# Output in token rows, and a base loaded in token rows and scaled by GpSimd, in a two-layer attention kernel

## What is computed

```python
# layer 0: per image, xn = group-normalised x, channels by tokens
q, k, v = Wq@xn + bq, Wk@xn + bk, Wv@xn + bv
out = softmax(q.T @ k) applied to v
y   = sigmoid(relu(mean(xn) @ se_w1.T) @ se_w2.T)     # one number per channel
x   = x + gamma*out + xn*y                            # the "base" is x + xn*y
# layer 1: tokens by channels
t = x as tokens (the image transposed)
t = t + softmax(n @ n.T) @ n                          # n = layer-normalised t
p = softmax(ln(t) @ router_w + router_b); the best 2 of 8 experts, renormalised
t = t + sum over the 2 experts of p_e * (ln(t) @ expert_w[e] + expert_b[e])
return t as image (transposed back)
```

## Time and profile before

| | |
|---|---|
| median of 3 runs | 2607.51 us (2606.56 to 2609.67) |
| span of the profiled execution | 2606.9 us |
| TensorE (PE) busy | 2524.8 us, 97% |
| VectorE (DVE) busy | 2123.7 us, 81% |
| ScalarE (ACT) busy | 1843.8 us, 71% |
| GpSimd (POOL) busy | 455.6 us, 17% |
| loads of x | 24 of 384 KB, 4.2 us from issue to landing |
| stores of y | 48 of 192 KB, 1.9 us |

### The profile page before, as it was taken

The page is one execution under the profiler, slowest core; times in us unless marked ns, Lnnn a source line. Parts: engine busy times, 40 slices in busy tenths (PEclk is TensorE's granted clock), DMA queues, the critical chain, the costliest instruction groups (busy, mean ns, idle before and its releaser), DMA issues.

```text
span 2606.9 us, 45676 instructions
## 1 busy us (share of the span) xinstructions
PE 2524.8 (97%) x15201; PEld 2325.1 (89%) x15201; DVE 2123.7 (81%) x6221; ACT 1843.8 (71%) x3598; POOL 455.6 (17%) x840
## 2 busy tenths in 40 slices
PE   6999999999999999999999999999999999999997
PEld 5889998899988999889988899889998899988996
DVE  6896789878888788887888878988779877898776
ACT  4667766777677776777766777667776777767775
POOL 0000221013210131101311014010240112300134
PEclk9999999999999999999999999999999999999998
DMA  1000000000000000000000000000000000000000
GB/s 39 1 19 1 4 10 1 22 4 7 7 1 22 4 7 7 16 8 4 10 4 22 1 4 10 4 22 1 4 10 4 22 1 4 13 1 4 1 10 13
DMA packets 11319, 23.12 MB, mean 9 GB/s; under 512 B 1360, under 2 KB 7760, under 8 KB 11088
## 3 DMA queue, kind: packets, MB, share of 16 engines
q1 hardware_dynamic: 11088, 20.20, 2.2%
HBM read 10.76 MB, written 9.44 MB: 8 GB/s over the span
## 4 chain that ended last, share of the span: by engine, by line
PE 72%; DVE 13%; ACT 8%; issue 5%; POOL 1%; DMA 1%; SPq 0%; ACTq 0%; POOLq 0%; DVEq 0%
PE ps L1193 19%; PE ps L1195 19%; PE ps L1194 19%; PE ps L1213 11%; DVE row_space L997 4%; ACT row_space L740 2%; DVE pt_lo L1012 2%; PE ps L1338 2%; ACT row_space L792 1%; DMA x_chan<-x 1%; DVE pt_lo L1092 1%; ACT pt_hi L751 1%; DVE t_tok L1030 1%; ACT pt_hi L801 1%; DVE xg_lo L957 1%
## 5 line engine op out<-in xcount | busy, mean ns | idle before, releaser
L751 ACT ACTIVATE pt_hi<-ps 128x384 fp32r<-128x384 f32 x864 | 419.9, 489 | 290.3 <-PE ps L1213 287.4
L1012 DVE TENSOR_TENSOR pt_lo<-ps,pt_hi 128x384 fp32r<-128x384 f32 x864 | 473.6, 551 | 108.7 <-ACT pt_hi L751 102.6
L997 DVE TENSOR_SCALAR_CACHE_REDUCE row_space<-ps,key_bias 128x512 f32<-128x512 f32 (+1 forms) x720 | 492.4, 690 | 52.8 <-PE ps L1195 48.4
L1213 PE MATMUL ps<-ident,row_space 128*128 128x128 f32 x2736 | 448.4, 273 | 20.9 <-ACT row_space L740 20.9
L740 ACT ACTIVATE row_space<-row_space,negmax 128x512 f32<-128x512 f32 (+2 forms) x432 | 403.0, 933 | 64.6 <-DVE negmax L1006 64.4
L1213 PEld LDWEIGHTS ps<-ident,row_space 128*128 128x128 f32 x2736 | 344.7, 141 | 105.0 <-ACT row_space L740 34.3
L1193 PE MATMUL ps<-pt_hi,v_hi 128*128 128x384 f32 x864 | 355.8, 412 | 8.4 <-ACT y_out L760 7.7
L1092 DVE TENSOR_TENSOR pt_lo<-row_space,pt_hi 128x768 fp32r<-128x768 f32 x260 | 251.0, 966 | 96.1 <-ACT pt_hi L801 96.1
L792 ACT ACTIVATE row_space<-ps,shift 128x768 f32<-128x768 f32 x260 | 233.9, 900 | 127.7 <-PE ps L1195 126.6
L1193 PE MATMUL ps<-pt_hi,tn_hi 128*128 128x384 f32 x864 | 304.6, 353 | 9.8 <-DVE pt_lo L1092 6.9
L1194 PE MATMUL ps<-pt_lo,tn_hi 128*128 128x384 f32 x864 | 292.5, 339 | 0.0
(11 more groups left out here) (210 smaller groups left out, 5453.6 us busy)
## 6 DMA issues: line engine op xcount, KB each, us to landing
x_chan<-x SPq DMA_DIRECT2D x24, 384.0 KB, 4.2
y<-y_out SPq DMA_DIRECT2D x48, 192.0 KB, 1.9
t_tok<-eb SPq DMA_DIRECT2D x1, 516.0 KB, 5.5
t_tok<-ew SPq DMA_DIRECT2D x1, 516.0 KB, 6.3
row_space<-wqkv SPq DMA_DIRECT2D x1, 192.0 KB, 3.3
se_sb<-se SPq DMA_DIRECT2D x1, 68.0 KB, 4.8
biases<-channel SPq DMA_DIRECT2D x1, 2.0 KB, 5.1
```

Source lines behind the costliest of these rows:

```text
L751: act.activation(pt_hi[:, slot, :], ring_bank(step)[:, 0:BW], ACT.Copy)\
L997: dve.tensor_scalar(row_part(n, r, a, w), ring_bank(step)[:, 0:w], key_bias[:, row:row + 1], None, ALU.add, ALU.max, accum_out=mx[:, row % ...
L1012: dve.tensor_tensor(pt_lo[:, slot, :], ring_bank(step)[:, 0:BW], pt_hi[:, slot, :], ALU.subtract).then_inc(pt_lo_ready, 1)
L1213: ins = pe.transpose(ring_bank(step)[:, k * 128:(k + 1) * 128], src(k), ident[:, :])
```

## The change

`x` is passed a second time as `tokens`, in token rows, laid out by the host. SP loads it straight into `t_tok`, in two parts (tiles 0 to 11 and 12 to 17), the first when the last `expert` of block 3 of the image before is done, the second when its last `o1add` is. GpSimd multiplies each block by the scale and adds the shift, in the place of `baset`. For that the two columns are turned into rows spread over all partitions: a new step `rows` (VectorE spreads them, TensorE transposes twice, ScalarE copies out). The steps `base` and the transposes and copies of `baset` are gone. The output is stored in token rows from `acc`, which now has two buffers; `yt` and `y_out` are gone, the -1 is put into the shift, and the host transposes the result. Loads of the next x wait for `xgnorm` in place of `baset`.

```diff
@@ EARLIER_BLOCK
-                 4: {4: [('expert', 2)], 9: [('scaled', 2)], 15: [('yt',)]}}
+                 4: {4: [('expert', 2)], 9: [('scaled', 2)]}}
@@ moe: the step yt and its slots (22, 35, 44, 49, 58, ...) are dropped
@@ PROJECT_SLOTS
-                 16: [('base', 0)], 18: ...
-                 22: [('base', 1)], 35: [('base', 2)]}
+                 16: [('rows', 0)], 18: ...
@@ FIRST_BLOCK
-FIRST_BLOCK = {0: [('fold', 0)], 1: [('fold', 1)], 4: [('fold', 2), ('foldsplit',)], 5: [('base', 0)], 8: [('base', 1)],
-               9: [('base', 2)]}
+FIRST_BLOCK = {0: [('fold', 0)], 1: [('fold', 1)], 4: [('fold', 2), ('foldsplit',)], 5: [('rows', 0)]}
@@ sync
+            def load_tokens(b, u):
+                tiles = slice(0, 4 * TPB) if u == 0 else slice(4 * TPB, NT)
+                sp.dma_start(t_tok[:, tiles, :], tokens[b][:, tiles, :]).then_inc(tokens_loaded[u], 16)
+
+            sp.wait_ge(e_split, 2)
+            load_tokens(0, 0)
+            load_tokens(0, 1)
+
             def store(b, mb):
-                sp.wait_ge(y_chan_ready, at(y_chan_ready, "yt", b, mb))
-                sp.dma_start(y[b, :, mb * BW:(mb + 1) * BW], y_out[:, out_buffer(mb), :]).then_inc(y_stored[out_buffer(mb)], 16)
+                sp.wait_ge(tile_added, at(tile_added, "scaled", b, mb, TPB - 1))
+                sp.dma_start(y[b, mb], acc[:, mb % 2, :, :]).then_inc(y_stored[mb % 2], 16)
             for b in range(B):
                 if b + 1 < B:
-                    sp.wait_ge(ring_full, filled(("baset", b, NB - 1)))
+                    sp.wait_ge(xg_norm_ready, at(xg_norm_ready, "xgnorm", b, LB - 1))
...
                 for mb in range(4):
                     store(b, mb)
                 if b + 1 < B:
+                    sp.wait_ge(expert_added, at(expert_added, "expert", b, 3, TPB - 1))
+                    load_tokens(b + 1, 0)
+                    sp.wait_ge(o1_added, at(o1_added, "o1add", b, NB - 1))
+                    load_tokens(b + 1, 1)
                     store(b, 4)
@@ gpsimd
+                if kind == "baset":
+                    m = step[2]
+                    t = t_tok[:, TPB * m:TPB * (m + 1), :]
+                    shape = [128, TPB, 128]
+                    pool.wait_ge(base_rows_ready, at(base_rows_ready, "rows", b, 0))
+                    pool.wait_ge(tokens_loaded[m // 4], 16 * (b + 1))
+                    pool.tensor_tensor(t, t, base_rows[:, 0, :].unsqueeze(1).broadcast_to(shape), ALU.mult)\
+                        .then_inc(base_scaled, 1)
+                    pool.wait_ge(base_scaled, at(base_scaled, *step))
+                    pool.tensor_tensor(t, t, base_rows[:, 1, :].unsqueeze(1).broadcast_to(shape), ALU.add)\
+                        .then_inc(base_tok_ready, 1)
@@ scalar: base, baset and yt dropped
+                elif kind == "rows":
+                    act.wait_ge(ring_full, filled(step))
+                    if b:
+                        act.wait_ge(base_tok_ready, at(base_tok_ready, "baset", b - 1, NB - 1))
+                    act.activation(base_rows[:, :, :], tiled(ring_bank(step)[:, 0:256]), ACT.Copy).then_inc(base_rows_ready, 1)
@@ vector
+                elif kind == "rows":
+                    if b:
+                        dve.wait_ge(ring_full, filled(("rows", b - 1, 0)))
+                    dve.tensor_copy(rows_src[:, :, :], gs[:, 9:11].unsqueeze(2).broadcast_to([128, 2, 128])).then_inc(rows_spread, 1)
@@ vector, expert, k == 0
-                        if b or m:
+                        if b or m >= 2:
-                            dve.wait_ge(ring_full, filled(("yt", *block_before(b, m))))
+                            dve.wait_ge(y_stored[m % 2], 16 * (b * (NB // 2) + m // 2))
@@ tensor
-                elif kind == "baset":
-                    m = step[2]
-                    pe.wait_ge(base_done, at(base_done, "base", b, m // 2))
-                    transpose3(step, lambda k: x_chan[:, m * BW + k * 128:m * BW + (k + 1) * 128])
+                elif kind == "rows":
+                    wait_ring(step)
+                    pe.wait_ge(rows_spread, at(rows_spread, *step))
+                    for k in range(2):
+                        ins = pe.transpose(ring_bank(step)[:, k * 128:(k + 1) * 128], rows_src[:, k, :], ident[:, :])
+                    ins.then_inc(ring_full, 1)
...
-                elif kind == "yt":
-                    m = step[2]
-                    pe.wait_ge(tile_added, at(tile_added, "scaled", b, m, TPB - 1))
-                    transpose3(step, lambda k: acc[:, k, :])
```

More of the change, by code:

```diff
@@ L113, in statistics, with moe @@
                                                   ("se_in", b), ("se_out", b)]
-def moe(b, m, norm, ut, router, experts, out):
-    s = {router: [("router", b, m)], router + 1: [("gates", b, m)], out: [("yt", b, m)]}
+def moe(b, m, norm, ut, router, experts):
+    s = {router: [("router", b, m)], router + 1: [("gates", b, m)]}
     if ut is not None:
@@ L267 @@
     "fold": ["ring_full", "bias_left"], "foldsplit": ["bias_folded", "e_hi_ready", "e_split"],
-    "xgnorm": ["xg_norm_ready"], "xg": ["xg_hi_ready", "xg_lo_ready"], "base": ["base_done"],
+    "xgnorm": ["xg_norm_ready"], "xg": ["xg_hi_ready", "xg_lo_ready"], "rows": ["rows_spread", "ring_full", "base_rows_ready"],
     "fuse": ["ring_full", "fused_hi_ready", "fused_ready"], "vproj": ["ring_full", "v_hi_ready", "key_bias_ready", "v_lo_ready"],
-    "baset": ["ring_full", "base_tok_ready"],
+    "baset": ["base_scaled", "base_tok_ready"],
     "qproj": ["ring_full", "q_hi_ready", "q_lo_ready"],
@@ L342, with build @@
 RING_BANK, BANK_BEFORE = ring_banks()
-def build(nc, x, wqkv, channel, se, ew, eb, y):
+def build(nc, x, tokens, wqkv, channel, se, ew, eb, y):
     ctx = ExitStack()
@@ L459, in build @@
         xg_lo_ready = signal("xg_lo_ready")
-        base_done = signal("base_done")
+        rows_spread = signal("rows_spread")
+        base_rows_ready = signal("base_rows_ready")
+        base_scaled = signal("base_scaled")
+        tokens_loaded = [signal(f"tokens_loaded{i}") for i in range(2)]
         fused_hi_ready = signal("fused_hi_ready")
@@ L657, in take @@
                     term = [term_of(m, k, i) for i in range(5)]
-                    total, paired = acc[:, k, :], at(terms_paired, *step) * 4 - 4
+                    total, paired = acc[:, m % 2, k, :], at(terms_paired, *step) * 4 - 4
                     pool.wait_ge(terms_ready, at(terms_ready, *step))
@@ L695, in take @@
                         .then_inc(xg_hi_ready, 1)
-                elif kind == "base":
-                    u = step[2]
-                    act.wait_ge(xg_norm_ready, at(xg_norm_ready, "xgnorm", b, LB - 1))
-                    cols = slice(u * LW, (u + 1) * LW)
-                    act.activation(x_chan[:, cols], x_chan[:, cols], ACT.Identity, bias=yshift, scale=yscale)\
-                        .then_inc(base_done, 1)
+                elif kind == "rows":
[3 more added lines that the diff above has]
+                    act.activation(base_rows[:, :, :], tiled(ring_bank(step)[:, 0:256]), ACT.Copy).then_inc(base_rows_ready, 1)
                 elif kind == "fuse":
@@ L1417 @@
         "x": np.asarray(x).reshape(B, C, NTOK),
+        "tokens": np.asarray(x).reshape(B, C, NT, TILE).transpose(0, 3, 2, 1),
         "wqkv": np.stack([np.asarray(L0_conv_Wq), np.asarray(L0_conv_Wk), np.asarray(L0_conv_Wv).T], axis=1),
@@ L1430 @@
         args.append(nc.dram_tensor(name, arrays[name].shape, F32, kind="ExternalInput").ap())
-    out = nc.dram_tensor("y", (B, C, NTOK), F32, kind="ExternalOutput").ap()
+    out = nc.dram_tensor("y", (B, NB, TILE, BW), F32, kind="ExternalOutput").ap()
     build(nc, *args, out)
     r = run_bass_kernel_spmd(nc, [arrays], core_ids=[0])
-    return r.results[0]["y"].reshape(B, C, 48, 48)
+    y = np.asarray(r.results[0]["y"]).reshape(B, NB, TILE, TPB, C)
+    return np.ascontiguousarray(y.transpose(0, 4, 1, 3, 2)).reshape(B, C, 48, 48)
```

83 lines of the change are left out of this document (28 added, 55 removed).

## The result

The changed kernel takes 2621.48 us (median, 2620.41 to 2625.37), the kernel before 2608.31 us in the same comparison: ratio 1.0053, 95% interval 1.0040 to 1.0065. It is slower by half a per cent, where 2595.0 was forecast, and outside the range. The profiled execution spans 2619.6 us against 2606.9, 12.7 us more.

A forecast was written before the change was run, and what follows sets the result against it. TensorE, busy 97% of the span, was taken to bound the kernel. Terms -29.5 + 1.8 + 17.3 + 3.8 - 5.9 = -12.5 us gave 2595.0 us, 0.5% faster, range 2583 to 2607.

The forecast's parts named there:

- The `rows` wait: Layer 1's slot 16, seven times: TensorE waits for VectorE's copy queued behind `p1low`; 17.3 us lost with the copy.
- In image 0: Block 1, slot 5: TensorE waits for `rows` behind VectorE's `pt` and reaches the same point 3.8 us later.
- 31.5 - 2.0 = 29.5 us: TensorE's saving from 96 removed `baset` and `yt` triples at 0.33 us, less 2.0 us lost to a wait.
- New pauses of TensorE in layer 0's attention: Sign given in advance: if TensorE gets new pauses in layer 0's attention, the prediction is wrong; no size given.
- the ring: PSUM banks given out in turn to steps; the prediction had no term for a changed turn, so 0 us.
- Layer 1, slots 44 to 53: Seven removed triples there were to save their full time on TensorE: -2.3 us.
- `yt` of block 5: Slot 22 of the next image: its removal only lengthens TensorE's wait for `p1low`; 6 x 0.33 = 2.0 us not saved.
- the last image and the tail: Last image's layer 1 and the end: removing `yt` saves 4.3 us before the router and 1.6 us at the store.
- the relief of ScalarE: ScalarE loses `base` and the `yt` and `baset` copies, at most 80 us together; counted as nothing because TensorE hides it.
- TensorE's busy time: Sign expected in the profile after, over the whole kernel: TensorE's busy time lower by some 45 us.
- the third one: Rival: GpSimd passes and VectorE hinder each other in 40 blocks of layer 0's attention; 22 us lost, 2617 us; chance 0.10.
- The second (VectorE takes over): Rival: VectorE sets the pace in layer 0's attention; 40% of 29.5 us lost, 2607 us, no change; chance 0.20.

The follow-up runs named there:

- e2: Changed kernel with the ring of PSUM banks turned by one place at slot 0 of block 5, images 1 to 6: 2619.91 us, ratio 1.0052.
- e4: Changed kernel with `xt_lo` made for 8 of 384 columns from image 1 on, less work for VectorE: 2617.39 us, ratio 1.0042.
- e5: Changed kernel with GpSimd's scale and shift passes done on 8 of 384 columns: 2618.95 us, ratio 1.0048.
- e7: Changed kernel with GpSimd's passes of blocks 2 to 4 moved to slot 6, ahead of the normalisation, all work kept: 2618.65 us, ratio 1.0044.
- e6: Kernel before with only one of three transposes of each `baset` kept: 2598.51 us, ratio 0.9968.
- e3: Changed kernel with `rows` split (VectorE's copy in slot 16, transposes in slot 18) and the bank ring turned back by one: 2593.18 us, ratio 0.9947.
- e10: e8 with the transposes `ut` of block 3 one slot earlier (47 for 48): 2585.16 us, ratio 0.9917.
- e8: Changed kernel with passes moved to slot 6, bank ring turned back, `rows` spread in slot 16 and transposed in slot 22: 2579.92 us, ratio 0.9897.
- e9: Changed kernel with `rows` added to the steps ahead of `p1low` in a slot, nothing else moved: 2604.40 us, ratio 0.9992.
- e11: e8 with GpSimd's two passes on 8 of 384 columns: 2581.26 us, ratio 0.9903.

## Why the prediction was wrong, step by step

- **The `rows` wait: the mechanism and the size were right.** The sum had 17.3 + 1.5 = 18.8 us for slot 16. The slot's cost in the five kernels that keep the step there was 22.3, 25.3, 28.6, 28.4 and 30.0 us with 2, 4, 6, 6 and 7 half clocks: 1.54 us for each, and 22.3 - 2 x 1.54 = 19.2 without any. What the term lacked is the clock: +3.1 us in the profile after, up to 10.8 in others. In image 0 a half clock follows too: +5.5 for 3.7 (+4.2 to +5.4 in e2, e4, e5 and e7 with the same pause).
- **The step that failed is "31.5 - 2.0 = 29.5 us" on the path,** with "TensorE sets the pace, VectorE is 5% behind" as its reason. (96 x 0.33 is 31.7 and not 31.5, which changes nothing.) The terms for layer 0 from image 0's block 2 to block 4 of the others had -20.1 us and got -6.3. Of the 13.8 that are missing, 7.8 are the passes beside the normalisation (2.7 in block 3 and 5.1 in block 4, shown by e5 and e7). 2.4 are block 2, where VectorE sets the pace at the head: e6 shows it without GpSimd, e4 gives it back by relieving VectorE. The rest, 3.6, is mostly at the boundary (2.4), where the head of block 1 waits 0.74 us for 0.39 in image 4 (distance of the starts less the usual 0.17). In e4 and e5 the boundary is as in the profile after to 0.2 us, so neither the passes nor `xt_lo` is its cause; nothing else was tried there, and it stays open. The prediction read 23.82 of 25.00 us as 5% to spare. Per block a triple is 0.33 us, and at the head all of VectorE's lateness counts at once. New pauses of TensorE in layer 0's attention were the prediction's own sign of being wrong, and they came: 28.8 us at the heads for 20.9 before.
- **A term that was put at nothing without a word: the ring.** +6.6 us, shown by e2 and e3. The diff removes and adds steps that take banks in turn, so every later step gets another bank. The prediction didn't look at who had each bank before. This was in the code and could have been read.
- **Layer 1, slots 44 to 53:** forecast -2.3, measured +2.1. `yt` of block 2 stood ahead of the router of block 3, which now waits 0.43 us for `u_lo` (L1105, image 3), and an expert product 0.27 us longer (by its turn in the ring, for its bank). That is read from the starts and was not tried by itself: e10 took the first wait away and brought another. It is the same case as `yt` of block 5, which the prediction did see.
- **Right:** `yt` of block 5 gave nothing back (+0.1); the last image and the tail (-8.4 for -8.3); token loads hidden (768 KB landed in 4.3 us, estimate 9.4); a pass at 1.01 us (taken 1.1); the relief of ScalarE worth nothing that I could find.
- **A sign that was wrong:** TensorE's busy time was to fall by some 45 us and fell by 17.2, and by 25.1 in e8. The 45 are the sum of the durations of what went, less the two transposes; the prediction itself says that durations overlap and are not the price.
- **Not forecast, on the good side:** block 5 of layer 0, -1.9 us. VectorE's wait for x before the statistics fell from 15.7 to 4.8 us, and TensorE's wait at the head of block 5 from 1.02 to 0.39 in image 4, by the starts. The prediction had said that TensorE doesn't pause there. That the earlier x is the cause is argued, not tried.
- **The rivals.** Neither of the two that VectorE is in was the whole. That the third one's time, 2617, lies near the measured 2621 is luck: a third of its 22 us came, and the rest of the distance is the ring, the clock and what else is named here. The second (VectorE takes over) had 11.8 us lost and some 6 came; the third (passes and VectorE hinder each other) had 22 and 7.8 came. It supposed one VectorE instruction held up in 40 blocks; it was two in each of the 14 blocks where `lnapply` meets a pass. They came together, with the ring and the clock on top: 13.8 + 6.6 + 3.5 (slot 16) + 1.8 (image 0) + 4.4 (slots 44 to 53) = 30.1 us lost against the forecast, less 1.9 (block 5), 1.5 (slots 26 to 44) and 1.0 (start): the 25.5 between -12.8 and +12.7, within the rounding. A range built of cases that exclude each other couldn't hold that.

On the hindrance, the rows show this: the one-input SBUF pass `lnapply` went from 350 to 502 ns in the mean, and the copy of `rows` takes 0.28 us alone and 0.54 beside GpSimd's adds; the low part of `pt`, which reads one input from PSUM, takes 550 ns in the mean in the 58 instructions that lie beside a pass and 552 in the 806 others. By the Trainium skill, SBUF — State Buffer, section "Who interferes with whom", a VectorE instruction in a two-port mode and a GpSimd instruction exclude each other for the whole of whichever came first; `lnapply` would have to be of that kind, which no run shows by itself. The trace agrees in what it shows: the 28 long normalisation instructions all end right behind a pass, and three of them together lost 1.55 us, one and a half passes of 1.01.

## What to carry over

Ask of an added wait first where the producer stands in its engine's queue: one word that put the copy ahead of a 1 us neighbour was worth 17 us in the medians. When a change removes or adds a user of a buffer ring, list who had each buffer before the critical step, in both kernels. GpSimd's passes cost nothing beside VectorE work that reads PSUM and held up the normalisation from SBUF to SBUF; put such work beside the first kind, and judge small edits by stretches of the trace while a pause with an uncertain clock behind it stands in the kernel.

## What the runs showed of the hardware

A pause of TensorE of 2.43 us was followed by 1.2 GHz in 23 of 30 cases, one of 2.02 us in 2 of 5, one of 4.95 us in 5 of 5 (the five kernels that keep the step in slot 16 behind `p1low`, one profile each; e9 adds a sixth of 4.95). In slot 16 a half clock cost 1.54 us. The kernel is the same from image to image, and so is the pause; what picks the ones that are hit stays open. GpSimd's passes, which read and write SBUF, left PSUM-reading VectorE instructions alone: 551 ns for the 80 low parts of `pt` that lie beside a pass in e8 and 551 for the 784 others, and 0.6 us between the spans of e8 and e11.
